# Gates spread over the partitions by DMA through DRAM in place of 128 matmuls with a constant

## The reference, cut to what matters

```python
x = x + cross_attention(ctx, ctx, layernorm(x), mask, W_merge, b_merge)      # 8 x 512 x 512
h = layernorm(x).reshape(4, 1024, 512)
rw = gates(h)                                      # per token: softmax over the chosen of 16 experts
q = einsum('bte,bted->btd', rw, einsum('btc,ecd->bted', h, q_proj))          # k and v the same way
attn = softmax(causal(q @ k.T / 8)) @ v            # heads of 64
mixed = attn[:, :, None, :] * rw[..., None]        # token x 16 experts x 64
x = x + einsum('bted,edc->btc', mixed, o_proj)
```

## Time and profile before

| | us |
|---|---|
| median of 3 runs | 1024.38 (1023.87 to 1027.03) |
| the profiled execution | 1025.62 |
| its span, first to last instruction | 1023.7 |
| PE busy | 950.0 (93%) |
| DVE busy | 622.2 (61%) |
| POOL, ACT busy | 257.9, 238.0 |
| first stage, tail behind the last expert product | 0 to 165, some 992 to 1024 |

### The profile page before, as it was taken

One profiled execution on the slowest core, in us unless ns is written; L12 is line 12 of the kernel. 1 busy time (PEld: TensorE's weight loads), 2 busy tenths in 40 slices (PEclk: granted clock), 3 DMA queues, 4 the chain that ended last, 5 costly groups with the idle time before them and its releaser, 6 DMA issues.

```text
span 1023.7 us, 16695 instructions
## 1 busy us (share of the span) xinstructions
PE 950.0 (93%) x5288; PEld 865.0 (84%) x5288; DVE 622.2 (61%) x1907; ACT 238.0 (23%) x575; POOL 257.9 (25%) x409
## 2 busy tenths in 40 slices
PE   4787867899999999999999999999999999999987
PEld 3455545899999999998999899989999999999975
DVE  6788763675656565656656565647474747574732
ACT  6676650121111111111112021212021111111211
POOL 4544445422121212121212031203030203021201
PEclk9788877999999999999999999999999999999998
DMA  5445422110101010102010101010101000000010
GB/s 171 148 174 180 182 89 107 52 63 1 62 1 62 2 62 1 62 2 62 0 62 0 53 10 58 4 52 11 52 11 52 11 31 31 32 31 32 21 40 22
DMA packets 30576, 53.70 MB, mean 52 GB/s; under 512 B 7241, under 2 KB 7241, under 8 KB 30386
## 3 DMA queue, kind: packets, MB, share of 16 engines
q1 hardware_dynamic: 30514, 53.01, 15.2%
HBM read 36.22 MB, written 16.78 MB: 52 GB/s over the span
## 4 chain that ended last, share of the span: by engine, by line
issue 38%; PE 31%; POOL 8%; POOLq 4%; DVE 2%; DMA 1%; ACT 0%; DVEq 0%; ACTq 0%
PE psQ L1290 19%; PE psO L1382 7%; POOL mixedT_lo L951 5%; POOLq L886 1%; POOLq L889 1%; PE psM L1367 1%; DMA mixed_f<-in_w_o 1%; PE psT L1262 1%; POOLq L891 1%; PE psQ L1382 1%; DVE acc L1148 1%; PE psT L1333 1%; POOL Wo_lo L935 0%; POOL probs L916 0%; POOLq L883 0%
## 5 line engine op out<-in xcount | busy, mean ns | idle before, releaser
L1290 PE MATMUL psQ<-Wqkv_hi,hT_hi 128*128 128x384 f32 x1024 | 354.5, 346 | 0.0
L1290 PE MATMUL psQ<-Wqkv_hi,hT_lo 128*128 128x384 f32 x1024 | 348.0, 340 | 0.0
L1290 PE MATMUL psQ<-Wqkv_lo,hT_hi 128*128 128x384 f32 x1024 | 347.9, 340 | 0.0
L1148 DVE SCALAR_TENSOR_TENSOR acc<-psQ,RW,acc 128x192 f32<-128x192 f32 x448 | 165.7, 412 | 230.4 <-PE psQ L1290 201.3
L1290 PEld LDWEIGHTS psQ<-Wqkv_lo,hT_hi 128*128 128x128 f32 x1024 | 194.0, 189 | 2.0
L1290 PEld LDWEIGHTS psQ<-Wqkv_hi,hT_hi 128*128 128x128 f32 x1024 | 193.9, 189 | 2.1
L1290 PEld LDWEIGHTS psQ<-Wqkv_hi,hT_lo 128*128 128x128 f32 x1024 | 193.2, 189 | 0.0
L951 POOL TENSOR_TENSOR mixedT_lo<-mixed_f,mixedT_hi 128x512 fp32r<-128x512 f32 x64 | 81.9, 1291 | 187.2 <-ACT mixedT_hi L1025 187.2
L1382 PE MATMUL psO<-Wo_hi,mixedT_hi 128*128 128x512 f32 x248 | 100.1, 404 | 2.2 <-POOL mixedT_lo L951 2.1
L1382 PE MATMUL psO<-Wo_hi,mixedT_lo 128*128 128x512 f32 x248 | 97.6, 394 | 0.0
L1382 PE MATMUL psO<-Wo_lo,mixedT_hi 128*128 128x512 f32 x248 | 97.5, 393 | 0.0
(11 more groups left out here) (183 smaller groups left out, 1386.5 us busy)
## 6 DMA issues: line engine op xcount, KB each, us to landing
X<-in_x SPq DMA_DIRECT2D x8, 1024.0 KB, 5.4
x_scratch<-XR SPq DMA_DIRECT2D x16, 512.0 KB, 2.9
X<-x_scratch SPq DMA_DIRECT2D x32, 256.0 KB, 2.7
resid<-x_scratch SPq DMA_DIRECT2D x32, 256.0 KB, 3.1
out<-resid SPq DMA_DIRECT2D x32, 256.0 KB, 2.1
stage<-in_w_qkv SPq DMA_DIRECT2D x8, 768.0 KB, 6.1
mixed_f<-in_w_o SPq DMA_DIRECT2D x8, 256.0 KB, 3.3
CTX<-in_ctx_in SPq DMA_DIRECT2D x8, 154.0 KB
```

Of the source, the lines that this page charges most:

```text
L1148: dve.scalar_tensor_tensor(out=acc[e][:], in0=src, scalar=w, in1=acc[e][:], op0=ALU.mult, op1=ALU.add).then_inc(expert_added, 1)
L1290: last = pe.matmul(psQ[g % 4][:, 0:PW], x[:, c * P:(c + 1) * P], w[:, c, g * PW:(g + 1) * PW], start=(c == 0 and m == 0), stop=(c == KC - ...
```

## The change

The matmuls with `spread` go, with the constant and the 16 POOL instructions that build it (L903 to L923, left out below). `gates_q` and `gatesT` keep the 16 experts once, in float32 and not as a high and a low part; the bank is transposed one slot earlier (slot 20 and 4) and DVE alone copies it out. SP stores the 16 x 256 gates in DRAM, waits until they are there, and loads them back with eight DMAs, each of which repeats two rows of 1 KB over 64 partitions (128 KB written in SBUF, 1 MB for the eight). In SP's list they stand ahead of the next tile's `X2` load, whose tile the statistics of slots 24 and 8 read. DVE's mix reads this `spread` in SBUF instead of a bank of `psT`. The mixes no longer take banks, so a body has 18 uses instead of 26.

```diff
-GATES_T_AT = {21: 0, 5: 1}
+GATES_T_AT = {20: 0, 4: 1}
-    gates_q = sb("gates_q", [P, (TILES + 1) * 64])
-    gatesT = sb("gatesT", [P, S], F32R)
-    spread = sb("spread", [P, OC, P], F32R)
+    gates_q = sb("gates_q", [P, TILES, E])
+    gatesT = sb("gatesT", [E, 2 * P])
+    spread = sb("spread", [P, OC, 2 * P])
+    gate_dram = nc.dram_tensor("gate_scratch", (B, 2, E, 2 * P), F32, kind="Internal").ap()
-    MOVES, HIS = 26, 18
+    MOVES, HIS = 18, 16
@@ SP @@
+            def spread_gates(b, h):
+                n = 2 * b + h
+                gate = gate_dram[bass.ds(b, 1), h].rearrange("a e l -> (a e) l")
+                sp.wait_ge(gatesT_out, n + 1)
+                sp.dma_start(gate, gatesT[:]).then_inc(st_gates, 16)
+                sp.wait_ge(st_gates, 16 * (n + 1))
+                for u in range(4):
+                    for r in range(2):
+                        sp.dma_start(spread[r * DH:(r + 1) * DH, 2 * u:2 * u + 2, :],
+                                     gate[4 * u + r:4 * u + r + 3:2, :].partition_broadcast(DH)
+                                     ).then_inc(spread_in[u], 16)
                     if lead and j == 0:
                         load_resid(b - 1, 2)
                         load_resid(b - 1, 3)
+                        spread_gates(b - 1, 1)
...
                     if qkv and j == 2:
                         load_resid(b, 0)
                         load_resid(b, 1)
+                        spread_gates(b, 0)
@@ POOL @@
-                        pool.tensor_tensor(twice, rw, inv, ALU.mult).then_inc(gates_divided, 1)
+                        pool.tensor_tensor(gates_q[:, i, :], RW[:, i, :], p_inv[i % 2][:].broadcast_to([P, E]),
+                                           ALU.mult).then_inc(gates_divided, 1)
@@ ACT @@
-                        act.activation(gatesT[0:GK, h * 2 * P:(h + 1) * 2 * P], psT[moves.bank()][0:GK, 0:2 * P], ACT.Copy
-                                       ).then_inc(moved_hi, 1)
+                        moves.step()
@@ DVE @@
-                        lo(gatesT[where], None, gatesT[where], lambda bank: bank[32:GK, 0:2 * P])
+                        n = moves.step()
+                        dve.wait_ge(moved, n)
+                        if not isinstance(ab, int) or ab + h >= 1:
+                            dve.wait_ge(st_gates, 16 * (2 * ab + h))
+                        dve.tensor_copy(gatesT[:], psT[moves.bank()][0:E, 0:2 * P]).then_inc(moved_lo, 1)
+                        dve.wait_ge(moved_lo, n)
+                        dve.sem_inc(gatesT_out, 1)
-                        dve.wait_ge(moved, moves.step())
+                        dve.wait_ge(spread_in[u], 32 * (2 * ab + h + 1))
-                                          psT[moves.bank()][:].rearrange("p (c l) -> p c l", c=2),
+                        dve.tensor_tensor(mixed_f[u % 2][:], spread[:, 2 * u:2 * u + 2, :],
                                           attT[h][:].unsqueeze(1).broadcast_to([P, 2, 2 * P]), ALU.mult
-                                          ).then_inc(moved_lo, 1)
+                                          ).then_inc(mixed, 1)
@@ PE @@
-                            last = pe.transpose(bank[:, place(s)], gates_q[:, (2 * h + s) * 64:(2 * h + s + 2) * 64],
+                            last = pe.transpose(bank[0:E, place(s)], gates_q[:, 2 * h + s, :],
                                                 ident[:])
-                        bank = next_bank(moved_lo, gates_in_place[h], has_high=False)
-                        for s in range(2):
-                            last = pe.matmul(bank[:, s * 2 * P:(s + 1) * 2 * P], spread[:, 2 * u + s, :],
-                                             gatesT[:, h * 2 * P:(h + 1) * 2 * P], start=True, stop=True)
-                        last.then_inc(moved, 1)
```

More of the change, by code:

```diff
@@ L697, in experts_block @@
     PW = 2 * Q3
-    GK = 32 + E
     sb, ps, sem, pair = alloc(whole)
@@ L767, in experts_block @@
     mix_hi, mix_lo = sem("mix_hi"), sem("mix_lo")
-    spread_made = sem("spread_made")
-    gatesT_zero = sem("gatesT_zero")
+    gatesT_out = sem("gatesT_out")
+    st_gates = sem("st_gates")
+    spread_in = [sem(f"spread_in{u}") for u in range(4)]
+    mixed = sem("mixed")
     projected = sem("projected")
@@ L896, in _ @@
             pool.wait_ge(eps_made, 1)
-            pool.memset(gates_q[:], 0.0).then_inc(spread_made, 1)
-            pool.memset(gatesT[:].bitcast(F32), 0.0).then_inc(gatesT_zero, 1)
             pool.memset(logitT[:], 0.0).then_inc(logitT_zero, 1)
             powers(0, 0)
[L903 to L923, removed]
             def body(b, qkv, lead, prep):
@@ L1009, in body @@
                     if attn and k in GATES_T_AT:
[L1010 to L1014, removed]
-                        act.activation(gatesT[0:GK, h * 2 * P:(h + 1) * 2 * P], psT[moves.bank()][0:GK, 0:2 * P], ACT.Copy
-                                       ).then_inc(moved_hi, 1)
+                        moves.step()
                     if attn and k in MIX_AT:
                         h, u = MIX_AT[k]
-                        act.wait_ge(moved_lo, moves.step())
+                        act.wait_ge(mixed, 2 * TILES * ab + 4 * h + u + 1)
                         if h == 1:
@@ L1031, in body @@
                         act.wait_ge(neg_max_ready, TILES * ab + i + 1)
-                        if isinstance(ab, int) and ab == 0 and i < 2:
-                            act.wait_ge(spread_made, 17)
                         act.activation(probs[i % 2][:, 0:(i + 1) * P], psM[:, 0:(i + 1) * P], ACT.Exp,
@@ L1197, in body @@
                         h = GATES_T_AT[k]
-                        where = (slice(32, GK), slice(h * 2 * P, (h + 1) * 2 * P))
-                        lo(gatesT[where], None, gatesT[where], lambda bank: bank[32:GK, 0:2 * P])
+                        n = moves.step()
[5 more added lines that the diff above has]
+                        dve.sem_inc(gatesT_out, 1)
                     if attn and k in MIX_AT:
@@ L1278, in body @@
                 h_moved = logits = None
-                probs_moved, gates_in_place = {}, {}
+                probs_moved = {}
                 for k in range(SLOTS):
@@ L1319, in body @@
                         h = GATES_T_AT[k]
-                        bank = next_bank(gates_divided, TILES * ab + 2 * h + 2)
+                        bank = next_bank(gates_divided, TILES * ab + 2 * h + 2, has_high=False)
                         for s in range(2):
-                            last = pe.transpose(bank[:, place(s)], gates_q[:, (2 * h + s) * 64:(2 * h + s + 2) * 64],
+                            last = pe.transpose(bank[0:E, place(s)], gates_q[:, 2 * h + s, :],
                                                 ident[:])
-                        last.then_inc(moved, 1)
[L1325 to L1330, removed]
-                        bank = next_bank(moved_lo, gates_in_place[h], has_high=False)
-                        for s in range(2):
-                            last = pe.matmul(bank[:, s * 2 * P:(s + 1) * 2 * P], spread[:, 2 * u + s, :],
-                                             gatesT[:, h * 2 * P:(h + 1) * 2 * P], start=True, stop=True)
                         last.then_inc(moved, 1)
```

4 lines of the change are left out of this document (removed).

## The result

| | before | after |
|---|---|---|
| median, us | 1024.12 (4 runs, 1022.03 to 1027.03) | 1047.25 (4 runs, 1045.46 to 1048.95) |
| ratio, 95% interval | | 1.022 [1.0199, 1.0242] |
| profiled execution | 1025.62 | 1048.91 |

A forecast was written before the change was run, and what follows sets the result against it. PE, busy 93% of the span, was taken to bound the kernel. Terms -2.6 + 18.2 + 10.2 + 0 + 3.0 - 1.3 = +27.5 us gave 1053.1 profiled, 1051.9 as median; forecast's own range 1045 to 1060, overall 1030 to 1063.

The forecast's parts named there:

- Part 1: In 15 halves, 60 pairs of removed matmuls leave PE's list at 0.24 us each: 14.4 us.
- Part 2: At each half's first projection PE arrives earlier but waits for POOL's low part: 11.8 us given back, 2.6 stay.
- Part 3: At slots 20 and 4, a third psT bank use makes the logits wait for DVE: 18.2 us.
- Part 4: Second and third mix, with two SBUF operands, and POOL hold each other up: 5.7 plus 4.5, 10.2 us.
- Rival A: No holding between DVE and POOL at the mixes: only +17.3, 1041.7 us; chance 0.18.
- Part 5: SP's extra store and eight loads per half are hidden, X2 with 1.9 us to spare: 0 us.
- Part 6: In the last half nothing hides the DMAs; the projection starts at 1010.7 instead of 1007.73: +3.0 us.
- Part 7: At the start, DVE's gate arithmetic is no longer slowed while POOL builds spread: -1.3 us.
- Rival E: PE's clock drops mid-run, matmuls of 384 columns 0.32 us apart; chance 0.04.

The follow-up runs named there:

- e3: Changed kernel, but DVE's mix reads the attention from PSUM bank psM instead of its SBUF copy; 1039.38 us, ratio 1.0134.
- e5: Kernel before the change, with each mix's two 256-column matmuls cut to one of 64 columns; 1024.33 us, ratio 0.9998.
- e1: Changed kernel with gate transposes back in slots 21 and 5 and the next X2 loaded ahead of the spreading loads; 1041.01 us, ratio 1.0159.
- e4: Changed kernel with the spreading loads issued for the first half alone, the gate stores kept; 1043.34 us, ratio 1.0161.
- e2: Changed kernel with gate transposes back in slots 21 and 5, X2 left behind the spreading loads; 1091.17 us, ratio 1.0644.
- e6: Kernel before the change, with POOL's low part ahead of the powers in the slot that has both; 1024.29 us, ratio 1.0.
- e7: e8 with gate transposes back in slots 21 and 5 and X2 loaded ahead of the spreading loads, as in e1; 1017.1 us, ratio 0.9935.
- e8: Changed kernel with mixes reading the attention from PSUM and POOL's low part ahead of the powers; 1027.58 us, ratio 1.0029.
- e10: e7 with half of the spreading loads issued by ACT instead of SP; 1014.02 us, ratio 0.9885.
- e9: e1 with half of the spreading loads issued by ACT instead of SP; 1039.67 us, ratio 1.0146.

## Why the prediction was right, by its steps

The mechanisms that were forecast are there: the bank wait, the gain that is given back at the projection, and the holding between DVE and POOL. That the sum came within 5 us of the measurement is in part luck, since parts 3 and 4 were taken too large and the tail too small, and part 2 fits for another reason than the one I gave.

**Part 1, matmuls -14.4: -14.0.** 60 slots fell from 2.35 to 2.12 us, read from the starts and not from the records of 288 ns.

**Part 2, given back 11.8: shown.** e3 has the mixes at full speed and its slots 27 and 11 are 11.8 us longer than before; e5 gives the same without any DMA, 8.0 of 8.8. So 14.0 - 11.8 = 2.2 us stay, for which I had taken 2.6, but not where I said. I had 0.17 of slack in each of 15 halves. There are only 14 such waits: slot 27 of body 7 takes 4.86 us before and after, its projection waits for nothing, and that half keeps its 0.94. In the others e5 keeps next to nothing. Most of the rest of the 2.2 lies in the loop's halves 0, where the chain itself started 0.37 us earlier, in e3 as in the changed kernel (first mix 3.67 us into slot 23, before 4.04). As e1 suggests, this is DVE catching up during the bank wait. I had not seen this effect.

**Part 3, bank wait 18.2: 16.2.** The mechanism and places are as forecast, and e1 takes them away exactly. Slot 20 grew by 1.14 to 1.28, slot 4 by 1.60 to 1.68, or 1.25 behind a loop turn. Mis-sized was the pair of gate transposes that leaves the next slot: 0.22 and not 0.14 us, 15 x 0.08 = 1.2; the other 0.8 is in the waits. In six halves PE waits for `gates_q` first, 3.5 us in all; that lies inside the bank wait.

**Part 4, holding 10.2: 6.1 to 7.9.** e3 is 7.9 us faster; by slots 27 and 11, 17.9 - 11.8 = 6.1. The second mix took 1.04 to 1.06 in place of 0.68 in all 15 halves ahead of the tail, as forecast, but it delays 14 projections: 14 x 0.37 = 5.2 us and not 5.7. Mis-sized was the third mix. It met the power in bodies 0, 1 and 7 alone, in 4 halves, and held it for 0.50: 2.0 us and not 4.5. The fourth mix, 1.66 to 1.76 us, cost nothing, as forecast. Rival A (no holding) is out. The Trainium skill (SBUF — State Buffer, Who interferes with whom) calls the ports that DVE and GpSimd share an exclusive lock. The trace agrees closely: the second mix ended at 346.02, 0.54 behind the low part's end (345.48), and the power at 348.57, 0.43 behind the mix's (348.14). Blocked for the whole of the first, they would have ended 0.68 and 0.57 behind, 0.14 later each.

**Part 5, DMAs at 0: shown in the middle** by e4. But the cover was thinner than forecast, and that it held was luck. The eight issues took 6.15 us in the loop and not 4.5, and in the halves 0 of bodies 2 to 6 `X2` landed only 0.13 to 0.32 us ahead of the statistics, where I had 1.9 (0.58 to 2.71 in the halves 1). One slot later the cover is gone (e2).

**Part 6, tail +3.0: +5.3.** From the gates' copy to the projection 12.0 us, before 7.45. I had 2.1 us for the store; SP's next issue came 3.36 us behind the store's (+1.1 with the issue), and the first loads took 3.95 us to the first mix. Without the loads the stretch is 7.57 us (e4). Two low parts under the mixes took 2.75. The stretch is 4.6 us longer than before; another 0.8 lies behind the projection's start, where 12 matmuls in place of 8 start 0.43 us apart or more.

**Part 7, start -1.3: not settled.** Slots 0 to 11 of body 0 took 33.3, 33.5 and 34.0 us in the three kernels in which POOL builds the constant (before, e5, e6), and 31.1 to 33.2 in the nine others (31.8 after). The sign holds for the changed kernel (31.8), but e7, e8 and e10, without the constant too, come within 0.4 us of the kernel before, so the size isn't settled.

**Not forecast:** slot 2 behind a loop turn, 0.2 to 0.5 us shorter in four bodies (-1.4). It goes with the spreading loads: slot 2 sums to 24.1 to 24.7 us over bodies 1 to 7 in the eight kernels that have them, and to 25.7 to 26.1 in the four that don't (before, e4, e5, e6). Why isn't known. The sum of the measured terms, -14.0 + 11.8 + 6.1 + 16.2 - 1.4 + 5.3 - 1.2 = 22.8 us, leaves 0.5 of the 23.3 between the profiled executions; slots 16 and 19 grew by 0.6. Rival E was wrong for this kernel, whose waits in the middle kept the clock; e1, e2 and e9, where 3, 13 and 2 such waits cost the clock, show that it was close.

## What to carry to other kernels

Work taken from the busiest engine is only worth what the chain behind its next wait allows: cut the work alone first (e5) and see where it is given back. In a ring of two buffers, count the uses between a producer and the next one; a use moved ahead by one slot can turn a free wait into 1.1 to 1.7 us each time. And if an operand moves from PSUM to SBUF, look at what the other engine does at that very moment: here the order of two POOL items and the source of one operand turned a loss of 2.2% into one of 0.3% (e8). The gain of 1.2% (e10) needed the bank wait gone as well, and `X2` loaded first. A last point is from e2: price a late load with the clock behind it, which here was nearly half of the cost.

## What the runs showed of the hardware

- A DVE instruction with two SBUF operands ran 0.68 us alone, 1.05 begun 0.78 us into a POOL subtraction of 1.29, and 1.66 to 1.76 at the start of one. A power of one element on POOL, 0.57 us, took 1.07 under such an instruction. With one operand in PSUM (e3) neither happened.
- PE's waits ahead of a projection, in the changed kernel and the eight made from it, up to 1000 us: all 43 of 0.8 to 1.63 us were followed by matmuls at 2.4 GHz; of 29 between 1.71 and 2.16 us, 18 were followed by 1.2 GHz, with five or more of the next 512-column matmuls 0.43 us apart in place of 0.23. In e2, where PE had waited 0.6 to 2.4 us for H just ahead of the projection, it was 13 of 14; in the other kernels, with at most 0.25 there, 5 of 15. In e1 waits of 1.7 us went either way.
- The store of 16 KB let SP go on 1.45 to 1.47 us behind its issue in 12 of 16 halves after the change, and 2.87 to 3.37 in the others, the last one among them. Why is open.
- A spreading load of 128 KB took SP 0.65 to 0.77 us to issue in most halves (eight took 5.2 to 5.3 us outside the loop, 6.15 inside it; up to 5.8 and 6.7 in single halves) and landed in 3.0 (median). Why the loop is slower is open.
- The first expert matmul, ahead of which lies little but the first stage that no edit touched, started at 168.2 to 172.2 us in the profiled executions, so that differences of a few us between kernels are better read in the middle than in the medians.
